# An expert layer on one core: gate and up columns with a gap, loaded 128 at a time, and weights asked for inside the experts' block

## What is computed

```python
logits = x @ gate.T                      # 4096 x 64 experts
topk_w, topk_i = top 6 of softmax(logits) within the best 3 of 8 groups
buf[e, slot] = x[tok]                    # 64 experts, 96 slots each
g = einsum("ech,emh->ecm", buf, Wg)      # m = 176
u = einsum("ech,emh->ecm", buf, Wu)
out = einsum("ecm,ehm->ech", silu(g) * u, Wd)
y = sum over k of out[slot of (token, k)] * topk_w
shared = silu(x @ Sg.T) * (x @ Su.T) @ Sd.T      # m = 352, all tokens
return x + y + shared
```

## Time and profile before

| | us |
|---|---|
| time, median of 3 runs | 789.44 (787.31 to 789.6) |
| the profiled execution's own time | 786.29 |
| its span, first to last instruction | 784.6 |
| PE busy in the span | 658.6 |
| DVE busy | 480.5 |
| POOL busy | 350.9 |
| ACT busy | 336.2 |

### The profile page before, as it was taken

One profiled execution on the slowest core, in us unless ns is written; L12 is line 12 of the kernel. 1 busy time (PEld: TensorE's weight loads), 2 busy tenths in 40 slices (PEclk: granted clock), 3 DMA queues, 4 the chain that ended last, 5 costly groups with the idle time before them and its releaser, 6 DMA issues. The chain is left out here.

```text
span 784.6 us, 16833 instructions
## 1 busy us (share of the span) xinstructions
PE 658.6 (84%) x6353; PEld 474.9 (61%) x6353; DVE 480.5 (61%) x1087; ACT 336.2 (43%) x636; POOL 350.9 (45%) x356
## 2 busy tenths in 40 slices
PE   1799999998799988999733999799999999896093
PEld 0366666666577666767511465458788788785072
DVE  3266766668878899989753999713333333342058
ACT  2377777767658777676521323112212222221000
POOL 5012222213533454343120745556777777657264
PEclk9899999999989999999965999899999999999555
DMA  8234443356563333331118100017999999994298
GB/s 234 27 59 84 79 81 67 70 87 103 102 103 72 69 71 58 49 63 36 35 40 238 46 0 1 0 50 185 239 240 238 235 240 249 264 263 54 28 333 313
DMA packets 112063, 94.26 MB, mean 120 GB/s; under 512 B 59760, under 2 KB 95856, under 8 KB 111984
## 3 DMA queue, kind: packets, MB, share of 16 engines
q1 hardware_dynamic: 96368, 74.57, 38.1%
q0 software_dynamic: 10240, 14.16, 9.9%
q10 hardware_dynamic: 5376, 4.46, 1.9%
HBM read 60.26 MB, written 24.50 MB: 108 GB/s over the span
## 5 line engine op out<-in xcount | busy, mean ns | idle before, releaser
L1229 POOL DMA_INDIRECT sum_d<-nz,targets x64 | 91.8, 1434 | 41.6 <-issue 17.2
L724 DVE TENSOR_REDUCE mx<-Sc 128x16 f32<-128x1024 f32 x64 | 78.2, 1222 | 34.5 <-PE Sc L401 34.2
L1056 PE MATMUL bank<-xnT,sgu_sb 128*128 128x512 f32 (+1 forms) x192 | 88.0, 608 | 11.8 <-PEq L1592 11.8
L1111 PE MATMUL bank<-xT,wgu_sb 128*88 128x96 f32 x1024 | 95.1, 246 | 0.3 <-ACT xT L1180 0.3
L1280 DVE TENSOR_TENSOR hid<-sil,bank 88x192 f32<-88x192 f32 x64 | 22.4, 350 | 113.0 <-ACT sil L1186 58.3
L1111 PEld LDWEIGHTS bank<-xT,wgu_sb 128*88 128x88 f32 x1024 | 89.3, 157 | 0.7 <-issue 0.5
L600 ACT COPY ET<-ring 128x512 f32<-128x512 f32 x128 | 68.9, 589 | 40.3 <-PE ring L413 37.7
L429 PEld LDWEIGHTS O<-vbd,ET 128*64 128x64 f32 x2048 | 66.5, 138 | 29.3 <-issue 16.7
L728 DVE TENSOR_TENSOR E<-Sc,mx 128x1024 f32<-128x1024 f32 x64 | 78.4, 1225 | 6.9 <-DVE mx L724 0.5
L413 PE MATMUL ring<-ident,E 128*128 128x128 f32 x512 | 69.7, 280 | 12.9 <-ACT E L639 12.9
L429 PE MATMUL O<-vbd,ET 128*64 128x34 f32 x2048 | 73.6, 225 | 3.6 <-ACT ET L600 3.0
(11 more groups left out here) (152 smaller groups left out, 1112.1 us busy)
## 6 DMA issues: line engine op xcount, KB each, us to landing
wgu_sb<-in_wgu_dram SPq DMA_DIRECT2D x64, 352.0 KB
wd_sb<-in_wd_dram SPq DMA_DIRECT2D x64, 176.0 KB
sum_d<-zeros SPq DMA_DIRECT2D x16, 524.0 KB, 6.4
y<-sum_d SPq DMA_DIRECT2D x16, 512.0 KB, 8.8
kbd<-kT SPq DMA_DIRECT2D x248, 32.0 KB, 2.1
X<-in_x_dram SPq DMA_DIRECT2D x8, 512.0 KB, 6.5
rows_d<-xhT SPq DMA_DIRECT2D x8, 512.0 KB, 3.0
out_dram<-X ACTq DMA_DIRECT2D x8, 512.0 KB, 4.9
```

Source lines behind the costliest of these rows:

```text
L724: nc.vector.reduce_max(mx[:, m % 2, :], sc, AX.X).then_inc(s_mx, 1)
L1056: last = nc.tensor.matmul(out[0:m, :], sgu[:, e, k * MS + m0:k * MS + m0 + m], xnT[:, e, TOK * g:TOK * (g + 1)], start=e == 0, stop=e == 1)
L1111: last = nc.tensor.matmul(GP[e % 2][0:MH, CAP * u:CAP * (u + 1)], wgu[:, j, 4 * MH * c + MH * u:4 * MH * c + MH * (u + 1)], xT[:, e % 2, c ...
L1229: pool.indirect_dma_start(w["sums"][e % 2], bass.IndirectOffsetOnAxis(ap=targets[:, e:e + 1], axis=0), outs[:, e % EB, :], None, compute_o ...
```

## The change

It does two things. First, the expert's gate and up columns: in memory on the chip each half of 352 columns becomes 384, gate in 0 to 175, a gap of 16 that POOL clears once, up in 192 to 367, and another gap. They are used in loads of 128, 128 and 112 columns: gate 0 to 127; gate 128 to 175, the gap and up 0 to 63; up 64 to 175. So `gate_up` has six products and not eight. The transfer that fills them has four runs of 704 bytes per partition where it had one of 2816. The hidden product has gate 0 to 127 in one piece of 128 rows and gate 128 to 175 in one of 48, so DVE takes three instructions (rows 0 to 63, 64 to 127, and 48 more) where it took one, with up's rows read at other partitions; and the down weights are kept as 128 and 48 rows, in three transfers where there was one.

Second, the two small blocks are gone. Their transfers and constants stand at the head of SP's and POOL's queues in the experts' block, with waits where the results are used.

```diff
+MU = 192
+MW = 2 * MU
+MR = M - 128
+    pieces = wgu[:].rearrange("p j (k m) -> p j k m", m=MU)
@@ SP
+            def up_weights(e):
+                j = e % EB
+                sp.dma_start(pieces[:, j, :, 0:M], w["wgu"][e].rearrange("p (k m) -> p k m", m=M)).then_inc(s_w[j], 16)
+
+            def down_weights(e):
+                j, cut = e % EB, 128 - MH
+                sp.dma_start(wd[0:MH, j, 0:E], w["wd"][e, :, 0:E]).then_inc(s_w[j], 16)
+                sp.dma_start(wd[MH:128, j, 0:E], w["wd"][e, 0:cut, E:2 * E]).then_inc(s_w[j], 16)
+                sp.dma_start(wd[0:MR, j, E:2 * E], w["wd"][e, cut:MH, E:2 * E]).then_inc(s_w[j], 16)
...
+            sp.dma_start(sgu[:], w["sgu"].rearrange("(c p) n -> p c n", p=128)).then_inc(s_in, 16)
+            sp.dma_start(sd[:, 0:2, :], w["sd"][0:256].rearrange("(c p) n -> p c n", p=128)).then_inc(s_in, 16)
+            sp.dma_start(sd[0:MS - 256, 2, :], w["sd"][256:MS]).then_inc(s_in, 16)
+            for j in range(EB):
+                up_weights(j)
+                down_weights(j)
             for e in range(NE):
                 if e + EB < NE:
                     sp.wait_ge(s_gu, e + 1)
-                    sp.dma_start(wgu[:, e % EB, :], w["wgu"][e + EB]).then_inc(s_w[e % EB], 16)
+                    up_weights(e + EB)
                     sp.wait_ge(s_d, e + 1)
-                    sp.dma_start(wd[:, e % EB, :], w["wd"][e + EB]).then_inc(s_w[e % EB], 16)
+                    down_weights(e + EB)
@@ PE
-                pe.wait_ge(s_w[j], 32 * (e // EB + 1))
+                pe.wait_ge(s_w[j], 64 * (e // EB + 1))
...
+                if e == 0:
+                    pe.wait_ge(s_wz, 1)
-                for u in range(4):
+                for u in range(3):
+                    m = min(128, MU + M - 128 * u)
                     for c in range(2):
-                        last = nc.tensor.matmul(GP[e % 2][0:MH, CAP * u:CAP * (u + 1)],
-                                                wgu[:, j, 4 * MH * c + MH * u:4 * MH * c + MH * (u + 1)],
+                        last = nc.tensor.matmul(GP[e % 2][0:m, CAP * u:CAP * (u + 1)],
+                                                wgu[:, j, MW * c + 128 * u:MW * c + 128 * u + m],
                                                 xT[:, e % 2, c, :], start=c == 0, stop=c == 1)
...
-                for u in range(2):
-                    last = nc.tensor.matmul(DP[e % 2][0:CAP, 0:E], hid[:, e % 2, u, :],
-                                            wd[:, j, E * u:E * (u + 1)], start=u == 0, stop=u == 1)
+                for u, m in enumerate((128, MR)):
+                    last = nc.tensor.matmul(DP[e % 2][0:CAP, 0:E], hid[0:m, e % 2, u, :],
+                                            wd[0:m, j, E * u:E * (u + 1)], start=u == 0, stop=u == 1)
...
-            pe.wait_ge(w["s_moe_in"], w["n_moe_in"])
+            pe.wait_ge(s_in, 48)
@@ ACT
-                nc.scalar.activation(sil[:, e % 2], GP[e % 2][0:MH, 0:2 * CAP], ACT.Silu).then_inc(s_esil, 1)
+                nc.scalar.activation(sil[:, e % 2], GP[e % 2][:, 0:2 * CAP], ACT.Silu).then_inc(s_esil, 1)
@@ POOL
+            nc.gpsimd.iota(slot[:], ...).then_inc(s_slot, 1)
+            nc.gpsimd.memset(pieces[:, :, :, M:MU], 0.0).then_inc(s_wz, 1)
+            nc.gpsimd.memset(own[:], 1.0).then_inc(s_one, 1)
+            nc.gpsimd.memset(lastone[:], 0.0).then_inc(s_one, 1)
+            nc.gpsimd.memset(lastrow[:], 0.0).then_inc(s_one, 1)
+            pool.wait_ge(s_one, 3)
+            for m, fill in ((own, 0.0), (lastone, 1.0), (lastrow, float(NT * 128 + CAP - 1))):
+                nc.gpsimd.affine_select(...).then_inc(s_one, 1)
             hidden(0)
@@ DVE
-                nc.vector.tensor_tensor(hid[:, e % 2].rearrange("p u s -> p (u s)"), sil[:, e % 2],
-                                        GP[e % 2][0:MH, 2 * CAP:4 * CAP], ALU.mult).then_inc(s_h, 1)
+                k, up = e % 2, GP[e % 2]
+                nc.vector.tensor_tensor(hid[0:64, k, 0, :], sil[0:64, k, 0:CAP], up[64:128, CAP:2 * CAP], ALU.mult)
+                nc.vector.tensor_tensor(hid[64:128, k, 0, :], sil[64:128, k, 0:CAP], up[0:64, 2 * CAP:3 * CAP], ALU.mult)
+                nc.vector.tensor_tensor(hid[0:MR, k, 1, :], sil[0:MR, k, CAP:2 * CAP], up[64:64 + MR, 2 * CAP:3 * CAP],
+                                        ALU.mult).then_inc(s_h, 1)
...
+            dve.wait_ge(s_slot, 1)
...
+            dve.wait_ge(s_one, 6)
@@ decoder_layer: the two small blocks are deleted
```

More of the change, by code:

```diff
@@ L989, in at_slot @@
         return k if e % 2 == 0 and k < len(LATE) else None
+    s_in = sem("shared_weights")
+    s_one = sem("columns")
+    s_wz = sem("gaps_cleared")
+    s_slot = sem("slots")
     s_up = sem("up")
@@ L1231, in scatter @@
                                         outs[:, e % EB, :], None, compute_op=ALU.add).then_inc(s_s[e % 2], 16)
+            nc.gpsimd.iota(slot[:], pattern=[[1, CAP]], base=0, channel_multiplier=0,
+                           allow_small_or_imprecise_dtypes=True).then_inc(s_slot, 1)
+            nc.gpsimd.memset(pieces[:, :, :, M:MU], 0.0).then_inc(s_wz, 1)
[4 more added lines that the diff above has]
+            for m, fill in ((own, 0.0), (lastone, 1.0), (lastrow, float(NT * 128 + CAP - 1))):
+                nc.gpsimd.affine_select(out=m[:], in_=m[:], compare_op=ALU.not_equal, fill=fill, base=-(CAP - 1),
+                                        pattern=[[0, 1]], channel_multiplier=1).then_inc(s_one, 1)
             hidden(0)
@@ L1454, in decoder_layer @@
         w = dict(gate=gate, x=x, ctx=ctx_rows, wq=wq, bq=bq, wk=wk, bk=bk, wv=wv, bv=bv, wc=wc, bc=bc, rows=rows_d,
-                 sums=sums_d, lasts=lasts_d, wgu=wgu, wd=wd, out=out)
+                 sums=sums_d, lasts=lasts_d, wgu=wgu, wd=wd, sgu=sgu, sd=sd, out=out)
         mem["keys"] = sb("keys", [128, NT * 64])
@@ L1514, in decoder_layer @@
         w["n_in"], w["n_x"] = 16 * 6, 16 * (NG - 1)
-        s_half = ctx.enter_context(nc.semaphore("const_half"))
         with nc.Block() as block:
@@ L1565, in decoder_layer @@
         w["sd_sb"] = sb("sd_sb", [128, 3, E])
-        w["wgu_sb"] = sb("wgu_sb", [128, EB, 8 * MH])
-        w["wd_sb"] = sb("wd_sb", [MH, EB, 2 * E])
+        w["wgu_sb"] = sb("wgu_sb", [128, EB, 2 * MW])
+        w["wd_sb"] = sb("wd_sb", [128, EB, 2 * E])
         w["s_w"] = [ctx.enter_context(nc.semaphore(f"expert_weights{j}")) for j in range(EB)]
-        s_iota = ctx.enter_context(nc.semaphore("router_constants"))
-        w["s_moe_in"] = ctx.enter_context(nc.semaphore("shared_weights"))
-        w["n_moe_in"] = 48
-        with nc.Block() as block:
-            @block.sync
-            def _(sp):
-                sp.dma_start(w["sgu_sb"][:], sgu.rearrange("(c p) n -> p c n", p=128)).then_inc(w["s_moe_in"], 16)
-                sp.dma_start(w["sd_sb"][:, 0:2, :], sd[0:256].rearrange("(c p) n -> p c n", p=128)).then_inc(w["s_moe_in"], 16)
-                sp.dma_start(w["sd_sb"][0:MS - 256, 2, :], sd[256:MS]).then_inc(w["s_moe_in"], 16)
-                for j in range(EB):
-                    sp.dma_start(w["wgu_sb"][:, j, :], wgu[j]).then_inc(w["s_w"][j], 16)
-                    sp.dma_start(w["wd_sb"][:, j, :], wd[j]).then_inc(w["s_w"][j], 16)
         moe = ExitStack()
@@ L1588, in decoder_layer @@
                             ("hT", [128, 3, TOK]), ("sh", [128, GT, E]), ("xg", [CAP, EB, E + NE]),
[L1589 removed]
+                            ("xT", [128, 2, 2, CAP]), ("sil", [128, 2, 2 * CAP]), ("hid", [128, 2, 2, CAP]),
                             ("wcol", [CAP, EB]), ("own", [CAP, 1]), ("lastone", [CAP, 1]), ("lastrow", [CAP, 1])):
             mem[name] = sb(name, shape)
[L1592 to L1604 removed]
         moe_phase(nc, ctx, mem, w)
```

14 lines of the change are left out of this document (removed).

## The result

The changed kernel is slower, by a little: 789.37 us (median of 20 runs, 785.82 to 793.48) beside 787.18 us (781.39 to 790.48) for the kernel before, a ratio of 1.0043 with an interval of 1.0024 to 1.0063. Forecast were 774.3 us and a range of 766 to 786. In its profiled execution the span is 787.4 us where it was 784.6.

A forecast was written before the change was run, and what follows sets the result against it. POOL's scatter and gather queue was taken to end the experts' stage, PE and DMA close, PE bounding before it. Terms -4.3 - 0.7 - 10.1 = -15.1 took the profiled 786.29 to 771.2, as median 774.3 us; range 766 to 786.

The forecast's parts named there:

- The blocks taken out: Start of the experts' block: PE released by the third shared-weight load, starting 4.3 us earlier; moved constants and waits cost nothing.
- Gate and up: On PE: 12 records at 82 ns instead of 16, -0.33 us per expert, if 128-column loads hide behind 96-column streams.
- wide loads: Rival: 128-column loads take 110 ns or more, PE gains nothing, POOL paced as before; 785.1 us, chance 0.05.
- The down product: On PE: keeps four records of 256 columns; weights of 128 and 48 rows change nothing in columns, so no cost.
- The 53 pairs: POOL's scatter and gather pairs up to the 54th scatter: 3.12 us each instead of 3.31, 165.4 us in all, -10.1.
- the floor of 2.98: POOL's own time per pair, read from two scatters that wait for nothing; 53 pairs would take 157.9 us.
- The first scatter -0.66: First scatter comes two gate and up groups after the first expert starts, so it moves 0.66 us earlier, once.
- The hidden product: On DVE: three instructions instead of one, +0.43 us per expert at most, hidden behind PE's work, so no cost.
- The transfers: Weight loads: 472 more packets per expert cost +0.23 us of DMA time, 2.91 us in all, below POOL's 2.98.
- The two sizes of the line: Packet price from 1024-byte packets at 47 ns and 256-byte at 17.6: 7.8 ns per packet, 0.038 per byte.
- Slower: Rival: DMA queues stay full, POOL's pairs take 3.77 us throughout, waiting for scatter e-2's landing; 808.8 us, chance 0.09.
- Clock: Rival: PE's idle time lowers its clock to 1.2 GHz for 20 experts, +18 us on the forecast, 792; chance 0.02.

The follow-up runs named there:

- one_block: The kernel before with only the two small blocks taken out: 784.29 us, ratio 0.9968 to the kernel before.
- loads_measured: one_block plus eight kinds of float32 products behind the last expert, in PE's idle tail, to measure weight loads: 784.66 us.
- down_128_rows: The changed kernel with both down products over 128 rows, the second padded with rows of zeros: 780.95 us, ratio 0.9926 to the kernel before.
- rows_paired: one_block plus six sets of products alternating between two row counts, behind the last expert's down product: 787.00 us in one run.
- three_of_four: one_block with the last quarter of gate and up left out (12 records per expert, outputs wrong): 781.78 us, ratio 0.9883 to the kernel before.
- no_loads: three_of_four without the weight loads of experts 8 to 63 (outputs wrong): 764.45 us, ratio 0.9723 to the kernel before.
- down_128_no_loads: down_128_rows without the weight loads of experts 8 to 63: 767.98 us in one run.
- pieces_only: one_block plus the change's 704- and 1024-byte rows in five transfers per expert, products unchanged: 783.42 us, ratio 0.9952 to the kernel before.

## Why the prediction was wrong

**The blocks taken out: right.** -4.3 was forecast, -4.0 came (10.15 to 6.16 us, from the block's first issue), and one_block shows it alone in the trace (6.05 us); in the time it is 0.3%, some 2.5 us, with an interval from none to 5. The landing of the third shared load was to release PE, and did. The costs put at nothing were nothing: POOL's constants and the clearing of the gaps (0.52 us) were done by 415.85, and no wait on them shows.

**Gate and up: the first step that failed.** "The trace has loads of 128 columns ... 60 ns apart, less than 82. So -0.33 us." Those four loads were for transposes, with `ident` beside them, and I took the price of a load from its columns without regard to the kind of product. Measured: some 67 ns for a transpose's load of 128 columns, 115 to 117 for an ordinary product's, over 64 rows and over 128 alike. "This holds if a load of 128 columns hides behind a stream of 96" was the right condition, and it doesn't hold: some 112 ns in the group against 81. The group went from 1.32 to 1.28 us, not to 0.99. The Trainium skill (TensorE: Matmul & The Clock Gate, LDWEIGHTS) gave 1.23, and I set it aside by the row of another kind; this case's products bear it out, with some 4 ns more each in the group ((1.28 - 1.23) / 12) and 4 to 10 ns more in the groups of loads_measured (77 and 117). It also says that rows don't count, and the 117 and 115 ns agree. The rival "wide loads" had this mechanism, at a chance of 0.05. It should have been the forecast for this term.

**The down product: the second, and the one that made the kernel slower.** "That their weights now have 128 and 48 rows changes nothing in columns" was true and beside the point. The crossing between 128 and 48 rows, and from 48 to the transposes' 96, costs (1.13 - 0.86) + (0.22 - 0.17) = 0.32 us per expert; down_128_rows takes it away and rows_paired shows it by itself. The experts of the trace of before have no load that crosses 64 rows, so the term should have had a bound above nothing. Its attention does cross, and I didn't look there: at 209 us, PEld has

```profile
209.68 0.64 PEld L401 LDWEIGHTS Sc<-kbd,qT 64*64 64x64 f32 x16
210.70 0.20 PEld L439 LDWEIGHTS ring<-ident,att 128*128 128x128 f32 x2 [0.39 <-issue]
```

At each of the 59 changes from L401's products (64 rows, 256 columns streamed) to loads over 128 rows between 60 and 380 us PEld stands idle for 0.38 us or more, and not where 128 rows follow 128 (L413 to L447). The number of weight columns changes there too, so it would have been a warning and not a proof. 2.63 us per plain expert is 2.35 - 0.04 + 0.32. Between experts 0 and 43 that is 43 x 0.28 = 12 us more on PE, of which the scatters show 7.1. The other 5 were at least in part slack: scatter 43 started 4.6 us after its rows had been weighed in the kernel before and 1.6 us in the changed one, and scatters 51 to 55 some 15 and some 10 us.

**The 53 pairs: the third, and it would have failed with a right PE too.** -10.1 us was forecast and +7.0 came. three_of_four has a group of 12 records in 1.15 us, just my PE, and POOL still took 3.37 us per pair and not 3.12. I argued that with POOL slower than PE the demand for weights falls to POOL's pace, and that shorter packets let a scatter's rows in sooner. No run shows the second. As to the first, even where POOL is the slower one the weights' traffic adds 0.2 to 0.4 us to a pair, as no_loads and down_128_no_loads show. So 3.12 was too near the floor of 2.98. "The first scatter -0.66" failed with gate and up: the stretch from PE's first product to scatter 0 went from 111.7 to 111.9.

**The hidden product: right.** Three instructions of 256, 249 and 256 ns where one took 350 ns, and PE waited 0.2 us for them in all.

**The transfers: right that they are cheap, too dear in size.** Forecast +0.23 us of DMA time per expert; the queue's packets took 0.14 more, and the time nothing (pieces_only). The two sizes of the line were also read in two ways, 47 ns from the bytes moved and 17.6 from the share; by the share both, 1024 bytes are 1.097 x 160 / 3504 = 50 ns, and the line gives 6.8 ns per packet and +0.20. The trace of before had no stretch with 704-byte rows.

**The rivals.** "Slower" came true in sign and not in mechanism: its place was the wait for scatter e-2's landing, which in the changed kernel is 3.7 us in 4 times. "Wide loads" gave 785.1, since it left the pace of POOL as it was; with the term of the rows it would have been 785.1 + 7 = 792, against 789.4 measured. Of the 2.7 us between them 2.3 are the scale: the median before was 789.44 in three runs and 787.18 in twenty. "Clock" did not happen in the changed kernel, whose PE was never idle between 560 and 720 us (1.00 in every stretch); in three_of_four it did, for two stretches at 0.91.

Put together, the forecast of 774.3 failed by the pairs above all: -10.1 us forecast, +7.0 measured, the change of sign by the down product's rows, and the missing gain by gate and up and by the weights' traffic. The sum as it should have been, against the profiled execution: -4.0 for the blocks, +0.2 up to scatter 0, +7.0 for the 53 pairs, -0.1 after them, which is +3.1 from the block's start (369.8 to 372.9), less 0.3 for an attention that ended 0.3 us sooner: 784.6 + 2.8 = 787.4.

## What to carry to other kernels

Take the price of a weight load from a row of the same kind of product, not from a transpose that has the same columns; a product whose stream is shorter than its load is bound by the load (here 81 ns against some 112), so merging columns saves little there. Keep neighbouring products on one side of 64 rows, and, as one change here suggests, of 32; pad with rows of zeros rather than cross. Before spending on the engine that is always busy, cut its work in an experiment and see whether the end moves: here the pairs of POOL's indirect transfers, beside DMA engines full of weights, got no shorter with a faster PE.

## What was not expected of the hardware

A float32 product of 256 columns takes 0.44 us behind one on the same side of 64 rows and 0.60 us behind one on the other side, as its weight load then starts only 0.36 us after the end of the load before; 48 rows next to 48, or next to 64, cost nothing, but 64 behind 32 cost the same 0.60 the one time that they met. Loads of 128 columns for transposes follow each other every 67 ns or so, those of ordinary products every 115 to 117. And a scatter and a gather of 96 rows took 2.99 us of POOL's time with the DMA engines at 0.45 of share, and 3.26 to 3.44 in the kernels that also loaded weights.
